# A scan layer and a mixture of experts in one kernel: scans of 1024 columns in two passes over channel halves, with one PSUM bank for the expert tiles

## The reference

```python
dt = softplus(xn @ dt_w.T + dt_b)                # [B, S, D]
A  = -exp(log_A)                                 # [D, N], N = 32
b, c = xn @ B_w.T + B_b, xn @ C_w.T + C_b        # [B, S, N]
h  = exp(A * dt_t) * h + (dt_t * x_t) * b_t      # over t, h is [B, D, N]
y  = sum_n(h * c_t) + D_skip * x_t
# mixture: 8 experts, top 2, at most 4096 tokens each, H = 1024
out_e = relu(x_e @ w1 + b1) @ w2 + b2            # weighted by the gates, added per token
```

## Time and profile before

| | |
|---|---|
| median of the runs | 4122.37 us |
| profiled execution | 4120.65 us, its span 4118.9 us |
| DVE busy | 3936.4 us, 96% of the span |
| POOL busy | 3437.9 us, 83% |
| PE busy | 3332.7 us, 81%; mean granted clock 0.925 of full |
| ACT busy | 2475.6 us, 60% |
| first scan | at 376.6 us |
| DMA | 507.55 MB, mean 123 GB/s |

### The profile page before, as it was taken

One profiled execution on the slowest core, in us unless ns is written; L12 is line 12 of the kernel. 1 busy time (PEld: TensorE's weight loads), 2 busy tenths in 40 slices (PEclk: granted clock), 3 DMA queues, 4 the chain that ended last, 5 costly groups with the idle time before them and its releaser, 6 DMA issues.

```text
span 4118.9 us, 76092 instructions
## 1 busy us (share of the span) xinstructions
PE 3332.7 (81%) x16264; PEld 2214.2 (54%) x16264; DVE 3936.4 (96%) x4036; ACT 2475.6 (60%) x5217; POOL 3437.9 (83%) x2340
## 2 busy tenths in 40 slices
PE   6787888888888887888888888888888888888886
PEld 3365555555555555555555555555555555555554
DVE  8797999999999999999999999999999999999997
ACT  2302666666666666666666666666666666666665
POOL 3003998999998999999999899999998999999997
PEclk8998999999999999999999999999999999999998
DMA  7973444445544444445544444445554544445554
GB/s 231 352 136 87 116 117 104 109 110 129 130 109 114 109 116 108 106 109 129 123 115 113 110 114 106 109 110 131 120 118 105 118 106 108 113 110 130 120 120 106
DMA packets 405053, 507.55 MB, mean 123 GB/s; under 512 B 71871, under 2 KB 243075, under 8 KB 404675
## 3 DMA queue, kind: packets, MB, share of 16 engines
q1 hardware_dynamic: 310854, 404.48, 35.6%
q0 software_dynamic: 68976, 84.86, 13.4%
q10 hardware_dynamic: 25104, 16.91, 1.7%
HBM read 381.48 MB, written 142.11 MB: 127 GB/s over the span
## 4 chain that ended last, share of the span: by engine, by line
DVE 32%; PE 18%; issue 16%; ACT 14%; POOL 7%; DVEq 4%; DMA 4%; SPq 4%; ACTq 0%; POOLq 0%
DVE h L1168 20%; ACT bank L746 12%; DVE hc L1152 10%; PE bank L610 9%; POOL u L948 4%; PE bank L571 4%; DVEq L1168 3%; PE bank L556 3%; POOL out_rows L908 2%; SPq L341 2%; DMA dt<-dt_rows 2%; DMA dt<-x 2%; PE bank L626 2%; SPq L328 1%; ACT ht L781 1%
## 5 line engine op out<-in xcount | busy, mean ns | idle before, releaser
L948 POOL TENSOR_TENSOR u<-dtx,b_sb 128x1024 f32<-128x1024 f32 x1024 | 2676.0, 2754 | 124.2 <-DVE h L1168 110.5
L1168 DVE TENSOR_TENSOR_SCAN h<-bank,carry,u 128x512 f32<-128x512 f32 x2048 | 2525.2, 1269 | 105.4 <-ACT bank L746 71.4
L746 ACT ACTIVATE bank<-dt,a_neg 128x512 f32<-128x512 f32 x2050 | 1414.6, 690 | 1049.0 <-DVE h L1168 989.1
L1152 DVE TENSOR_TENSOR hc<-h,bank 128x1024 f32<-128x1024 f32 x1024 | 1225.8, 1197 | 0.0
L610 PE MATMUL bank<-xgt,w_sb 128*128 128x256 f32 x4096 | 1085.8, 424 | 57.0 <-ACT ht L781 41.4
L571 PE MATMUL bank<-hc,rsum 128*32 128x512 f32 x4096 | 615.0, 676 | 617.6 <-DVE hc L1152 615.7
L610 PEld LDWEIGHTS bank<-xgt,w_sb 128*128 128x128 f32 x4096 | 853.3, 214 | 447.3 <-issue 317.9
L626 PE MATMUL bank<-w_sb,ht 128*128 128x256 f32 x4096 | 980.4, 394 | 0.0
L626 PEld LDWEIGHTS bank<-w_sb,ht 128*128 128x128 f32 x4096 | 776.7, 195 | 316.1 <-issue 215.2
L781 ACT ACTIVATE ht<-bank,b_sb 128x256 f32<-128x256 f32 x1024 | 423.4, 464 | 237.3 <-PE bank L610 231.9
L571 PEld LDWEIGHTS bank<-hc,rsum 128*32 128x32 f32 x4096 | 83.2, 111 | 758.7 <-DVE hc L1152 727.3
(11 more groups left out here) (109 smaller groups left out, 1965.6 us busy)
## 6 DMA issues: line engine op xcount, KB each, us to landing
dt<-dt_rows SPq DMA_DIRECT2D x528, 128.0 KB, 3.7
dtx<-dtx_rows SPq DMA_DIRECT2D x528, 128.0 KB, 2.9
b_sb<-bc_rows SPq DMA_DIRECT2D x520, 128.0 KB, 3.3
c_sb<-bc_rows SPq DMA_DIRECT2D x520, 128.0 KB, 3.5
w_sb<-w SPq DMA_DIRECT2D x18, 1024.0 KB, 6.5
dt_rows<-dt_n SPq DMA_DIRECT2D x136, 128.0 KB
dtx_rows<-dtx_n SPq DMA_DIRECT2D x136, 128.0 KB
out_rows<-y_sb POOLq DMA_DIRECT2D x133, 128.0 KB, 3.9
```

Of the source, the lines that this page charges most:

```text
L746: act.activation(a_ps[dh], dt[:, g, :], ACT.Exp, scale=a_neg[:, bass.ds(col, 1)]).then_inc(a_ready, 1)
L948: pool.tensor_tensor(u[:, 2 * i:2 * i + 2, :], dtx[:, 2 * gp:2 * gp + 2, :], b_sb[:, odd, k // 4, :].unsqueeze(1).to_broadcast([P, KD, HALF]),
L1152: dve.tensor_tensor(hc[:, 2 * (k % HB):2 * (k % HB) + 2, :], h[:, 2 * k % HR:2 * k % HR + 2, :], c_ps.unsqueeze(1).to_broadcast([P, KD, HA ...
L1168: dve.tensor_tensor_scan(h[:, (2 * k + dh) % HR, :], a_ps[dh], u[:, 2 * (k % UB) + dh, :], carry[:, bass.ds(hh % 2, 1), bass.ds(ng * 2 * N ...
```

## The change

- A scan tile has 1024 tokens, a whole sequence, and starts from 0.0; `carry` is gone. h, u, b, c, dt and dtx tiles are twice as long and half as many. A step is still a 128th of the work: one sequence, one half of the channels (`gh`, 4 groups), two groups of states: 8 scans of 1024.
- The decays go to two pairs of banks (2-3 and 4-5), c to bank 6. What is left for the expert tiles, the turned slots and the preparation is bank 7. `free(f)` on PE lets a fill start when the one before is emptied; `filled(f)` is ACT's wait for the fill. The order of the fills is up 0 to 3, preparation, down (both halves), turned slots.
- A weighing covers four groups of 512 columns, and there are four a step; those of the second group of states are made in the next step.
- The product dt*x moves from POOL to DVE, behind scan 1. The log `zl` is in SBUF. dt is prepared one chunk further ahead, so the prologue has one round more.
- The gate product and the copies of the gather and scatter indices move from POOL to ACT. y goes out in two additions for half a sequence each. w1 and w2 have one buffer.

```diff
-        a_ps = [bank[:, 2, :], bank[:, 3, :]]
-        c_ps = bank[:, 4, :]
-        m_ps = [bank[:, 5, :], bank[:, 6, :]]
+        a_ps = [bank[:, 2 + 2 * i:4 + 2 * i, :].rearrange("p b c -> p (b c)") for i in range(2)]
+        c_ps = bank[:, 6, :]
+        m_ps = bank[:, 7, :].rearrange("p (c s) -> p c s", s=SL)
...
-        z_ps = bank[:, 7, 0:KD * Q]
...
-        zl_ps = bank[:, 7, KD * Q:2 * KD * Q].rearrange("p (k t) -> p k t", k=KD)
+        z_ps = m_ps[:, 0, :]
+        bc_ps = m_ps[0:2 * N, 1, 0:Q]
...
+        FZ, FD, FT, FS = HC // 2, HC // 2 + 1, HC // 2 + 2, HC // 2 + 3
```

TensorE, a step:

```diff
+                    def free(f):
+                        pe.wait_ge(evac_done, st * FS + f + 2)
+                        settle(pe)
...
+                    moe_up(0)
+                    moe_up(1)
+                    quad(0)
+                    moe_up(2)
+                    moe_up(3)
+                    if ng == 0:
+                        y_turned(0)
+                    quad(1)
+                    prepare()
+                    if ng == 0:
+                        skip(0)
+                        y_turned(1)
+                    moe_down()
+                    quad(2)
+                    if ng == 0:
+                        skip(1)
+                    pe.wait_ge(xg_in, 16 * SJ * (st + 2))
+                    free(FT)
+                    turn_slots((s + 1) % 2)
+                    quad(3)
```

ScalarE, a step:

```diff
+                    def filled(f):
+                        act.wait_ge(fill_done, st * FS + f + 2)
+                        settle(act)
...
+                    def prep_out():
+                        filled(FZ)
+                        evac_z(p)
+                        evac_bc(p).then_inc(evac_done, 1)
+
+                    def down_out():
+                        act.wait_ge(o_scattered, 16 * SJ * (st + 1))
+                        act.wait_ge(gate_ready, st + 2)
+                        filled(FD)
+                        for j in range(SJ):
+                            ins = act.activation(o_sb[:, s % 2, j, :], m_ps[:, j, :], ACT.Copy, scale=gate[:, j:j + 1])
+                        ins.then_inc(evac_done, 1)
...
+                    for k in range(NG):
...
+                        act.wait_ge(scan_done, st * NG + k + 1 + SCAN0)
+                        decay(tk, (JPS * tng + tk // GPP) * NQ + tgh * GPP + tk % GPP)
+                        if k == 0:
+                            up_out(0)
+                            c_copy(1)
+                            gates_in()
+                        if k == 1:
+                            up_out(1)
+                        if k == 2:
+                            up_out(2)
+                            c_copy(2)
+                            if ng == 0:
+                                y_down(0, 4 * st + 1 + NSUM0)
+                        if k == 3:
+                            up_out(3)
+                            if ng == 0:
...
+                                y_up(0, 1 - gh, 2 * hf + 1)
+                            lay_gather()
+                        if k == 4:
+                            prep_out()
+                            if ng == 0:
+                                y_down(1, 4 * st + 2 + NSUM0)
+                            act.wait_ge(evac_done, st * FS + FZ + 3)
+                            softplus(p)
+                            c_copy(3)
+                        if k == 5:
+                            if ng == 0:
+                                y_up(1, 1 - gh, 2 * hf + 2)
+                        if k == 6:
+                            down_out()
+                            c_copy(0)
+                            log_part(p)
+                        if k == 7:
+                            slots_in(st * FS + FT + 2)
+                            lay_scatter()
```

SyncE, where the one w1 buffer is refilled, and VectorE and GpSimd:

```diff
+                    if s == SPE - 1:
+                        sp.wait_ge(fill_done, st * FS + HC // 2 - 1 + 2)
+                        settle(sp)
+                        sp.wait_ge(w1_in, 16 * (e + 1))
+                        settle(sp)
+                        load_w1((e + 1) % E)
...
-                dve.scalar_tensor_tensor(out=dt_n[:], in0=zv[:], scalar=0.0, in1=zl_ps,
+                dve.scalar_tensor_tensor(out=dt_n[:], in0=zv[:], scalar=0.0, in1=zl[:],
                                          op0=ALU.max, op1=ALU.add).then_inc(dt_done, 1)
...
+            with dve.Fori(0, STEPS) as st:
+                for k in range(NG):
+                    dve.wait_ge(u_ready, st * NG + k + 2)
+                    dve.wait_ge(a_ready, st * NG + k + 2)
...
+                    dve.tensor_tensor_scan(h[:, k, :], a_ps[k % 2], u[:, k % UB, :], 0.0,
+                                           ALU.mult, ALU.add).then_inc(scan_done, 1)
+                    if k % 2 == 0:
+                        weigh(st, k // 2)
+                    if k == 1:
+                        dtx_part(NG + 1 + st, ((st + 1) // NG + 1) % 2, (st + 1) % NG)
+                prep_dt(NG + 2 + st)
+            weigh(STEPS, 0)
+            weigh(STEPS, 1)
...
+                        pool.wait_ge(scan_done, st * NG + k - UB + 1 + SCAN0)
+                        pool.tensor_tensor(u[:, k % UB, :], dtx[:, gp, :], b_sb[:, j, :], ALU.mult).then_inc(u_ready, 1)
...
+                        if k < SJ:
+                            gather(st + 1, (s + 1) % 2, k)
+                        if k in (4, 5):
+                            scatter(st, (s + 1) % 2, k - 4, 2 * b + ng if adds else None)
```

More of the change, by code:

```diff
@@ new lines, in _ @@
+                    store_dt(NG + 1 + st, seq1 % 2, q1)
+                    store_dtx(NG + 1 + st, seq1 % 2, q1)
+                    next_b(0)
+                    if last:
+                        next_dtx(0)
+                        next_dtx(1)
+                    next_c(1)
+                    if last:
+                        next_dtx(2)
+                        next_dt(0)
+                        next_dtx(3)
+                    next_b(1)
+                    if last:
+                        next_dt(1)
+                        next_dt(2)
@@ L666, in _, with add_skip @@
-            pe.wait_ge(yt_ready, 2 * B + 1)
-            turn_y()
+            def add_skip(par, gh, th):
+                pe.matmul(y_ps[:, th, :], dskip_m[:, gh, :],
+                          xnt[:, bass.ds(par, 1), gh, th * HALF:(th + 1) * HALF].rearrange("p a t -> p (a t)"),
+                          start=True, stop=True, skip_group_check=True).then_inc(sk_used, 1)
+            for p in (NG, NG + 1):
+                prep(p, 1, p - NG)
+            pe.wait_ge(map_ready, 1)
+            pe.wait_ge(bcv_done, NG + 2)
@@ L748, in slots_in, with decay @@
+            def decay(k, col):
+                act.activation(a_ps[k % 2], dt[:, k % GPP, :], ACT.Exp, scale=a_neg[:, col:col + 1]).then_inc(a_ready, 1)
             def slots_in(value):
                 act.wait_ge(fill_done, value)
-                act.activation(xgt[:].rearrange("p k s -> p (k s)"), m_ps[TURN % 2], ACT.Copy).then_inc(evac_done, 1)
-            def y_down(value):
+                act.activation(xgt[:].rearrange("p k s -> p (k s)"), bank[:, 7, :], ACT.Copy).then_inc(evac_done, 1)
@@ L842, in _ @@
+            act.wait_ge(hc_done, 4 * STEPS + 2)
+            act.activation(c_ps, c_sb[:, 1, HALF:S], ACT.Copy).then_inc(c_ready, 1)
+            act.wait_ge(y_out, 16 * 2 * B)
+            for th in range(2):
+                y_down(th, 4 * STEPS + th + 1 + NSUM0)
+                y_up(th, 1, 2 * 2 * B + th + 1)
         @block.gpsimd
         def _(pool):
-            start_at_one(pool, u_ready, prep_done)
+            start_at_one(pool, u_ready)
             pool.wait_ge(consts_in, 16 * 8)
@@ L982, in _ @@
             for j in range(SJ):
[L983 removed]
+                scatter(STEPS, 1, j, None)
             pool.wait_ge(o_scattered, 16 * SJ * (STEPS + 2))
[L985 to L988 removed]
+            for th in range(2):
+                pool.wait_ge(y_evac, 2 * 2 * B + th + 2)
+                add_y(2 * B - 2 + th, th)
+            pool.wait_ge(y_out, 16 * (2 * B + 2))
```

726 lines of the change are left out of this document (312 added, 414 removed).

## The result

The changed kernel takes 4409.36 us (median of four runs, 4403.29 to 4413.45) against 4122.15 (4119.00 to 4123.99). The ratio is 1.0696, with a 95% interval of 1.0678 to 1.0715: 7% slower. The forecast was 4180, in a range of 4080 to 4250. The sign was right, the size was not: 229 us are missing.

A forecast was written before the change was run, and what follows sets the result against it. DVE bounded the old kernel; after the change, the bank 7 chain plus the wait for POOL: 128 steps of 29.45 us plus 7.3 from 381.9, then 18 behind, span 4176.8, forecast 4180 us, range 4080 to 4250.

The forecast's parts named there:

- the work of DVE: DVE's scans, weighings, product and dt instruction in each step: 26.9 us, 1.3 less than before.
- the chain through the one bank: Fills through bank 7 end with ACT's log at 28.2 us, so DVE waits before prep_dt; period 28.6 us.
- lock-free case: Rival at prep_dt: the two-operand instruction does not wait for POOL; periods 28.6 and 29.6, 4103 us; 20%.
- the lock: At prep_dt: two SBUF operands make DVE wait for POOL's running product; taken as 0.8 us a step.
- The upper bound of the forecast: At prep_dt: the wait for POOL costs at most 2.35 us, one u product.
- SP's loads are the same bytes in the same number: SP's load queue: the change leaves bytes and load count as before; listed under what costs nothing.
- land within a microsecond of their use, at places where two decays are in stock: dt tiles of a fourth step arrive within a microsecond of use, with two decays in stock; listed as costing nothing.
- 0.34 us of DVE: Product dt*x of 256 columns, behind scan 1: adds 0.34 us to DVE's step.
- up to 3 us of delay: Single w1 buffer, refilled late each sixteenth step: first fill delayed up to 3 us, 14 us at worst, taken as 0.
- the first scan: Start of the loop: one more preparation round, 5.3 us with the product, puts the first scan at 381.9 us.

The follow-up runs named there:

- e7: Changed kernel with the log moved earlier (k = 5) and SP's loads of b and dtx ahead of the product's store, dt loads moved forward: 4131.53 us.
- e5: Changed kernel with the loop's dt instruction reading its second operand from PSUM (c bank) instead of SBUF: 4389.35 us.
- e6: Kernel before the change with only its log written to SBUF instead of PSUM: 4487.88 us beside 4118.03.
- e12: Changed kernel with the loop's product dt*x back on GpSimd, behind its fourth u product: 4296.89 us.
- e4: Changed kernel with SP issuing b and, in ng = 3, the first dtx tile ahead of the product's store, dt loads moved forward: 4319.28 us.
- e11: e4 with b and c loaded in the loop at half length, 512 of 1024 columns: 4262.74 us.
- e10: e7 plus ACT's and PE's loops written out over 16 steps instead of 8, and w1 loaded earlier: 4077.45 us beside 4124.95.
- e15: e10 with the product dt*x back on GpSimd, measured in rounds: 4054.49 us, ratio 0.9838 to the kernel before.
- e8: Changed kernel with ACT's and PE's loops written out over 16 steps instead of 8, so half the jumps: 4402.01 us.

## Why the prediction was wrong

**Right: the work of DVE.** Forecast 2.19 us for a scan of 1024, 2.17 for a weighing of 2048 and 26.9 a step; e7 has whole steps at 26.91.

**Right: the chain through the one bank.** The log's end was forecast at 28.2 and is at 28.36 in the step shown; the medians for `ng` = 1, 2 and 3 are 28.35, 28.37 and 28.64. The forecast for the lock-free case, 28.6, was 0.6 low: e5 gives 29.2. The missing part lies behind the log. From its end to the next scan 0.78 us pass in e5, and the forecast had 0.1 for the handing over and 0.33 for the instruction, the distance that it takes in a row of others without a stop.

**Right in kind, wrong in size: the lock.** DVE's two-operand instruction does wait for POOL: 420 to 423 ns in every case with a PSUM operand, up to 2127 without. The forecast took 0.8 a step; in `ng` = 1 and 2 it is 0.2 to 0.3. Chain low and lock high cancelled, which is luck and the reason why 29.3 to 29.6 came out. The upper bound of the forecast, one product of 2.35 us, doesn't hold either: e7 has 3.5 us and e6 4.4.

The Trainium skill (SBUF — State Buffer, section "SBUF: two separate sides") says that a VectorE instruction with two SBUF inputs and a GpSimd instruction that reads SBUF exclude each other for the whole instruction. The trace agrees, with the numbers just given.

**Wrong: "SP's loads are the same bytes in the same number".** They are not. Each b and c row is loaded once for each channel half, 1024 DMAs and 134 MB more. This follows from the diff, where `load_bc` is called with `jj` over both halves, and the forecast counted dt and dtx, which stay at 528 each, and not b and c. The rest of that sentence fell with it: the dt tiles "land within a microsecond of their use, at places where two decays are in stock". ACT stops over 4 us for them in most `ng` = 3 and `ng` = 0 steps, and the two decays in stock guard DVE alone. What the decay holds up on ACT is `xgt`, and behind it all of PE's step.

**Wrong: an instruction moved was priced on its engine alone.** The product was taken as 0.34 us of DVE. Its place sets when SP may store it, and SP's queue holds all loads behind that store. e12 measures the whole: 113 us, of which 20 to 40 by DVE. The forecast had named, for POOL, who waits for an instruction, and did not ask it for SP.

**Wrong by omission: w1 and the jump.** The single w1 buffer was "up to 3 us of delay", taken as 0; PE waited 69.9 us in 7 times, up to 11.2. The jump of PE and ACT was in no sum, and the trace of the kernel before gave little sign of it: three such stalls of PE's up fills, up to 5.2 us, from 600 to 3900 us, and none on ACT above 0.6.

How the 234 us between the two spans (4176.8 and 4410.7) divide, with each step measured on top of the one before: SP's order 93 (e4, span 4317.6), the b and c bytes 57 more (e11, span 4261.1). Of the 84 that then remain, s = 0 (36.2 against 29.6, seven times) and s = 8 (32.3, eight times) hold 68, for which e10 against e7 points to w1 and the jump; the first scan, 5 us later in e11 than forecast, and the 5 us more behind the last step's start hold most of the rest. In e10 nothing waits for w1 any more and s = 0 is still at 36.3, with the jump before it. The split between w1 and the jump at s = 0 was not measured: no run goes without the jump there. Nor does the division stand alone: order, product and bytes all act on the same late tiles, and in another sequence each would get another share (the bytes alone 72, the product alone 113).

## What to carry to other kernels

Count every load again when the loops are reordered, by how often each row is fetched: the tiles that don't carry the new index are the ones fetched twice. Price a moved instruction by all who wait for it, a DMA queue above all: a store that waits at the head of a queue delays every load behind it. And a stock in front of the bounding engine guards only that engine; ask what else stands behind the late instruction on its own engine. Last, a mend can enlarge what is left: with the log early, DVE comes to its two-operand instruction while POOL is still behind, and waits longer for it.

## What the runs showed of the hardware

- A DVE instruction with both operands in SBUF can be held for more than one POOL instruction. Where POOL's products follow one another without a gap it isn't let in between them: 4.3 us (median of 104), where products last 2.3 to 3.3 (e6). In e15 it is held for up to 5.7 us, and in 15 cases two products begin while it waits. Every such record above 0.9 us ends 0.28 to 0.30 us behind the end of a product.
- When PE and ACT jump back in a loop body of 8 or 16 such steps, PE stands still for 4.3 to 6.5 us and ACT for up to 6.8 (e7, e10). It goes with the jump and with packets of kind `instruction`, one of 16 KB in q8 some 3.3 us before PE goes on and one of 8 KB in q14 some 2.2 us before ACT does. With fewer bytes loaded beside it PE's stop is shorter: 2.9 to 3.5 us (e11) in place of 4.1 to 5.6 (e4). It costs little where the engine would wait anyway (e8).
- An up fill takes 1.97 us, and 3.75 behind such a standstill of 5 us: the granted clock is 0.50 to 0.52 there, its level of 1.2 GHz, and 1.00 at the fast fill, 2.4 GHz.
- A wait that shrinks doesn't pay its length: e4 took 210 us off ACT's waits for dt and 90 off the time, e12 156 and 113.
